# Softmax order, load order and fp16 channel matmuls in a vision-transformer tower on one core

## The chip, the core and the metric

One NeuronCore of a Trainium2 chip runs the whole program. The metric is the device time of one execution in microseconds; lower is better. The kernel before was run three times: 1566.47, 1568.02 and 1568.35 us, median 1568.02.

## The reference

Sixty-four images of 2 x 104 x 104 pixels become 170 tokens each (169 patches and a class token) of 128 channels. All of it is float32:

```
normed = (concat(x, 4 shifted copies) - mean) * rsqrt(var + EPS)      # per image
h = conv(normed * gamma + beta, W, stride 8) + b ; cls token in front
x_enc = layernorm(h)
m = relu(gcn(x_enc, W1, b1))          # graph over 128 channels, 1 -> 4 channels
g = gcn(m, W2, b2)                    # 4 -> 4 channels
h = h + concat(x_enc, g) @ Wp.T + bp
h = h + ffn(layernorm(h))             # causal attention with 2 heads, then 8 gated experts
```

The program folds the second graph convolution and the four channels of Wp into one 128 x 512 matrix (`gcn_m`), so the graph part is: one product with the adjacency, four ReLUs (one for each channel, with its own scale and bias), and a sum of one product with Wp's plain part and four products with `gcn_m`.

## The kernel before

**Tiles.** The 64 images are 16 groups (`G`) of 4 images (`NB`). A group is T = 680 token columns on 128 partitions (channels). Matmul operands are mostly split in two fp16 parts, high and low, and a product is three fp16 passes (high x high, high x low, low x high); a matmul over 680 columns is two instructions of 340 (helper `both`, L764). The products with `gcn_m` are float32 (L764 too; operand `h1`, four ReLU outputs of 680 columns).

**Stages.** A first stage (until about 162 us) loads the images, multiplies 65 times with gamma on VectorE (L1217), convolves in 65 steps on TensorE (L751) and, woven between by the step numbers in `FIRST_0`, `GRAPH_0`, `QK_0` and `FIRST_1`, does the chains of groups 0 and 1 up to their attention. Then for each group follow `attention(g)` and `ffn(g)`. The experts run in 32 slots (`SLOTS`) and three slots behind (`LAG`): slot s does `experts_in(s)` (6 matmuls, L979), and `experts_out(s - 3)` (6 matmuls, L998). ScalarE writes a GELU and, in three slots of four, its fp16 high part (L625, L630). VectorE computes the low part (L1388; in every fourth slot also the high part, L1386), and after every fourth `experts_out` it weighs the expert's output with the gate (`weigh`, L1401), whereupon GpSimd adds it to the output in DRAM by an accumulating DMA (L458). `experts_out` of the next expert waits for `weigh`'s two halves (`half_ready`, `tmp_ready`).

**Order.** Each engine runs its own program in order, written out by hand: the dictionaries at the top of the file name the slot in which a step of the next groups is done (`LN2_SLOTS`, `QK_SLOTS` for group g+1, `EARLY_SLOTS` for group g+2). In slots 28 to 31 ScalarE does the four ReLUs (L546) of group g+2. In slots 31 to 34 TensorE does the attention values of group g+1 (L876), which ScalarE copies out of PSUM (`values_evac`, L579).

**Attention before.** TensorE: values, scores 0 (images 0 and 1, L891 and L895), `plain` and channel 0, scores 1, channels 1 and 2, then transposes (`turn_probs`, L906), channel 3, `weigh` (L918, probabilities times values), `project` (L925), `mean2`, gate logits (L961). VectorE: maxima 0 and 1 (L1295, L1298), `normalise` of each image (L1303, L1310), `turned` (L1317, the copy of transposed probabilities), `h2` (L1263, the sum of the graph part into the tokens), `y_parts`, `dev2`. ScalarE: 16 exponentials (L589), four for an image. The last group's attention has no graph part of a next group beside it (`ahead` is false).

**Loads.** SP loads the first images (`all0`, `all1`) and `pack_b`, ScalarE's queue `edge` and `pack_a` (gamma and the convolution's weights). In the first group GpSimd also splits the weights of experts 4 to 7 (`split`, L422 and L424), each time ahead of the accumulating DMA.

## Time and profile before

| | us |
|---|---|
| median of 3 runs | 1568.02 |
| the profiled execution, its time | 1570.0 |
| its span, first to last instruction | 1568.2 |
| first stage, until the first scores | about 164 |
| the period of one group in the middle | 87.73 |
| the last attention and its experts | about 85 |

In that execution TensorE is busy for 1489.1 us, VectorE 1192.9, ScalarE 1102.4 and GpSimd 191.8. The mean granted clock of TensorE is 0.985 of full speed. In the timeline a row is a run of equal instructions: start, time, engine, line, operation, output and inputs, count, and in brackets the idle time before it and what ended it. A float32 matmul shows as two records. Ends of matmuls are modelled, so the distance between starts is the better measure of TensorE's pace.

### The profile page before, as it was taken

To read this page: it belongs to the slowest core of one execution; us is meant where nothing else is said; L and a number is where in the kernel's file an instruction comes from. 1 tells how busy PE (TensorE), PEld (TensorE's weight loads), DVE (VectorE), ACT (ScalarE), POOL (GpSimd) and SP (SyncE) were. 2 spreads that over 40 slices of the span, in tenths; PEclk is the share of its full clock that TensorE was granted. 3 is DMA by queue.
4 is the path that set the end of the run, shared out by engine and by line. 5 is a ranking of instruction groups with operands and counts; after the bars stand their busy time and mean duration, and the time that the engine had idled before them with its cause. 6 is when DMAs were issued, how large, how long until landed. Compare 5 with 4: busy or idle time off the path is not lost.

```text
span 1568.2 us, 31340 instructions
## 1 busy us (share of the span) xinstructions
PE 1489.1 (95%) x10879; PEld 1021.1 (65%) x10879; DVE 1192.9 (76%) x2535; ACT 1102.4 (70%) x1925; POOL 191.8 (12%) x223
## 2 busy tenths in 40 slices
PE   6898999999999999999999999999999999999998
PEld 4554666666666666666666666666666666667665
DVE  6768886868778687878788787878788787877765
ACT  5232776777777777777777777787777777777766
POOL 1134041110101010110101010110101010100101
PEclk9998999999999999999999999999999999999979
DMA  7866043433333242433333242433333242433334
GB/s 237 197 152 137 25 138 46 107 45 98 38 93 48 34 109 36 107 45 98 44 89 47 43 97 36 107 44 98 44 98 44 55 83 32 108 43 101 53 90 54
DMA packets 40196, 125.55 MB, mean 80 GB/s; under 512 B 5728, under 2 KB 5728, under 8 KB 37984
## 3 DMA queue, kind: packets, MB, share of 16 engines
q0 software_dynamic: 22464, 55.81, 25.4%
q1 hardware_dynamic: 17408, 68.52, 12.6%
q10 hardware_dynamic: 288, 0.77, 0.1%
q8 instruction: 19, 0.31, 0.1%
q14 instruction: 17, 0.14, 0.0%
HBM read 68.98 MB, written 50.48 MB: 76 GB/s over the span
## 4 chain that ended last, share of the span: by engine, by line
PE 52%; DVE 23%; issue 6%; ACT 2%; DVEq 1%; DMA 1%; POOL 0%; POOLq 0%; ACTq 0%
PE pair L998 20%; PE pair L979 17%; PE pair L764 5%; DVE area L1388 5%; DVE area L1310 3%; PE pair L891 2%; DVE root_t L1230 2%; DVE area L1317 2%; DVE area L1401 2%; PE pair L925 1%; PE pair L918 1%; DVE area L1386 1%; PE pair L876 1%; PE pair L845 1%; PE pair L792 1%
## 5 line engine op out<-in xcount | busy, mean ns | idle before, releaser
L625 ACT ACTIVATE area<-pair,pack_b_sb 128x680 f32<-128x680 f32 x512 | 422.5, 828 | 225.9 <-PE pair L979 221.5
L1388 DVE TENSOR_TENSOR area<-area 128x680 f16<-128x680 f32 x512 | 444.7, 872 | 145.1 <-ACT area L630 140.3
L998 PE MATMUL pair<-area,ws 128*128 128x340 f16 x3072 | 529.9, 307 | 16.4 <-DVE area L1401 15.5
L979 PE MATMUL pair<-area,ws 128*128 128x340 f16 x3072 | 527.9, 308 | 0.0
L998 PEld LDWEIGHTS pair<-area,ws 128*128 128x128 f16 x3072 | 284.8, 98 | 172.1 <-DVE area L1401 47.3
L979 PEld LDWEIGHTS pair<-area,ws 128*128 128x128 f16 x3072 | 297.8, 98 | 143.8
L630 ACT ACTIVATE area<-pair,pack_b_sb 128x680 f16<-128x680 f32 x384 | 316.1, 823 | 0.0
L458 POOL DMA_DIRECT2D tower_out<-area x128 | 109.3, 854 | 1182.1 <-DVE area L1401 1112.4
L1401 DVE SCALAR_TENSOR_TENSOR area<-pair,pack_b_sb,area 128x340 f32<-128x340 f32 x256 | 133.9, 565 | 31.7 <-PE pair L998 23.0
L589 ACT ACTIVATE area<-pair,nbias,root 85x85 f32<-85x85 f32 (+1 forms) x256 | 112.3, 463 | 21.5 <-DVE nbias L1298 21.5
L751 PE MATMUL pair<-area,pack_a_sb 128*128 128x392 f32 (+1 forms) x260 | 95.9, 514 | 17.5 <-DVE area L1217 14.4
L751 PEld LDWEIGHTS pair<-area,pack_a_sb 128*128 128x128 f32 x260 | 50.8, 205 | 54.6 <-DVE area L1217 26.6
L1386 DVE CAST area<-area 128x680 f16<-128x680 f32 x128 | 67.3, 526 | 20.9 <-ACT area L625 15.5
L764 PE MATMUL pair<-area,gcn_m 128*128 128x340 f32 x256 | 81.6, 451 | 0.0
L1295 DVE TENSOR_REDUCE mx<-pair 85x4 f32<-85x340 f32 x64 | 41.0, 680 | 46.0 <-PE pair L895 46.0
L546 ACT ACTIVATE area<-pair,pack_b_sb 128x680 f32<-128x680 f32 x64 | 59.1, 934 | 16.6 <-PE pair L764 16.0
L1217 DVE TENSOR_TENSOR area<-area,pack_a_sb 128x728 f32<-128x728 f32 x65 | 61.7, 995 | 0.3 <-PE pair L751 0.3
L906 PE MATMUL pair<-ident,area 85*85 85x85 f32 x384 | 45.6, 257 | 13.2 <-DVE area L1310 13.2
L1310 DVE TENSOR_SCALAR area<-area,rs 85x85 f32<-85x85 f32 (+1 forms) x256 | 55.6, 278 | 2.3
L764 PEld LDWEIGHTS pair<-area,gcn_m 128*128 128x128 f32 x256 | 46.0, 190 | 17.0
L526 ACT ACTIVATE ht<-pair 128x392 f32<-128x392 f32 (+1 forms) x26 | 19.8, 874 | 50.1 <-PE pair L751 50.1
L589 ACT ACTIVATION_READ_ACCUMULATOR area<-pair,nbias,root 85x1 f32 x256 | 54.2, 212 | 0.0
(209 smaller groups left out, 1615.3 us busy)
## 6 DMA issues: line engine op xcount, KB each, us to landing
tower_out<-area POOLq DMA_DIRECT2D x128, 340.0 KB, 4.6
area<-gate_scratch SPq DMA_DIRECT2D x16, 1360.0 KB, 10.0
area<-gate_scratch SPq DMA_DIRECT2D x16, 1020.0 KB, 7.2
area<-cells SPq DMA_DIRECT2D x16, 392.0 KB, 5.2
area<-cells POOLq DMA_DIRECT2D x14, 392.0 KB, 6.5
area<-area POOLq DMA_DIRECT2D x14, 392.0 KB, 4.8
tower_out<-ht SPq DMA_DIRECT2D x16, 340.0 KB, 2.3
area<-gate_scratch SPq DMA_DIRECT2D x16, 340.0 KB, 4.8
```

Source lines behind the costliest of these rows:

```text
L458: pool.dma_start(out[:, g * T:(g + 1) * T], tmp[e % 2], accum_op=ALU.add).then_inc(out_done, 16)
L589: nc.scalar.activation(probs[:, b * SCORE + o0:b * SCORE + o0 + w], score_ps_at(b)[:, h, c * QC:c * QC + w], ACT.Exp, bias=nbias[:, n:n + ...
L625: nc.scalar.activation(two(hid[slot % NHID]), halves(hid_ps[slot % 2]), ACT.Gelu_apprx_tanh, bias=col(COL_B1 + slot)).then_inc(hid_ready, 1)
L630: nc.scalar.activation(two(hh[slot % NPART]), halves(hid_ps[slot % 2]), ACT.Gelu_apprx_tanh, bias=col(COL_B1 + slot)).then_inc(hhi_act, 1)
L751: last = mm(cells_ps(p, j), conv_w[:, shift * D:(shift + 1) * D], xg[n % XG][:, c0 * BZ:c1 * BZ], start=(shift == 0), stop=(shift == SHIFT ...
L764: last = mm(fr_ps[:, j, 0:TH], lhs, rhs[:, j, :], start=start, stop=stop)
L979: last = mm(hid_ps[slot % 2][:, j, 0:TH], lhs[:, w], rhs[:, j * TH:(j + 1) * TH], start=(i == 0), stop=(i == 2))
L998: last = mm(eo_ps[:, j, 0:TH], lhs[:, w], rhs[:, j * TH:(j + 1) * TH], start=(m % CH == 0 and i == 0), stop=(m % CH == CH - 1 and i == 2))
L1310: last = v.tensor_scalar(p, p, rs[:, n:n + 1], None, ALU.mult)
L1386: v.tensor_copy(hh[slot % NPART], hid[slot % NHID]).then_inc(hhi_dve, 1)
L1388: v.tensor_tensor(hl[slot % NPART], hid[slot % NHID], hh[slot % NPART], ALU.subtract).then_inc(hlo_ready, 1)
L1401: v.scalar_tensor_tensor(tmp[e % 2][:, j * TH:(j + 1) * TH], eo_ps[:, j, 0:TH], b2_s[:, e:e + 1], gbc[:, e * T + j * TH:e * T + (j + 1) * ...
```

## The change

1. The four channels' products are three fp16 passes over `gcn_h`, `gcn_l` (a new split of `gcn_m`, VectorE, once) and `h1_h`, `h1_l`. ScalarE writes a ReLU to one of two buffers (`relu`), and VectorE makes the high part and the low part of it (steps `part0` to `part3`).
2. Scores 0 and 1 of the next group are computed in slots 32 and 33, VectorE's maxima too; the values come after `plain` and channel 0, into another PSUM pair (`eo_ps`), and VectorE copies them out, in two copies.
3. `pack_a` is loaded in two parts on SP's queue.
4. GpSimd issues the accumulating DMA ahead of `split`.

The diff, cut to its core:

```diff
-               "relu0": 28, "relu1": 29, "relu2": 30, "relu3": 31}
+               "relu0": 28, "relu1": 29, "relu2": 30, "relu3": 31,
+               "part0": 29, "part1": 30, "part2": 31}
 FIRST_0 = ...
-           "relu2": 19, "relu3": 19}
+           "relu2": 19, "relu3": 19, "part0": 19, "part1": 19, "part2": 20, "part3": 20}
 FIRST_1 = ...
-           "relu2": 62, "relu3": 62}
+           "relu2": 62, "relu3": 62, "part0": 62, "part1": 62, "part2": 63, "part3": 64}
-DVE_PREP = {4: 1, 6: 2, 9: 3, 17: 5, 18: 6, 20: 7, 25: 8, 28: 9}
+DVE_PREP = {4: 1, 6: 2, 9: 3, 17: 5, 18: 6, 20: 7, 21: 8, 25: 9, 28: 10}
+        h1_h, h1_l = (h1[:, 2 * n * T:2 * (n + 1) * T].bitcast(F16) for n in range(2))
+        relu = [xh, sqq]
 # SP
+            sp.dma_start(gam, pack_a[:, 0:SHIFTS * NP * NP]).then_inc(gam_in, 16)
             sp.dma_start(all0, first0).then_inc(all0_in, 16)
+            sp.dma_start(conv_w, pack_a[:, SHIFTS * NP * NP:]).then_inc(conv_w_in, 16)
             sp.dma_start(all1, first1).then_inc(all1_in, 16)
 # GpSimd, weigh
+                    pool.dma_start(out[:, g * T:(g + 1) * T], tmp[e % 2], accum_op=ALU.add).then_inc(out_done, 16)
                     if g == 0 and e + 4 < E:
                         split(e + 4)
-                    pool.dma_start(out[:, g * T:(g + 1) * T], tmp[e % 2], accum_op=ALU.add).then_inc(out_done, 16)
 # ScalarE
-            act.dma_start(packs["pack_a"][:, :], pack_a).then_inc(pack_a_in, 16)
+                    if later or c >= 2:
+                        act.wait_ge(relu_lo, 4 * g + c - 1)
-                    nc.scalar.activation(two(h1[:, c * T:(c + 1) * T]), halves(fr_ps), ACT.Relu,
+                    nc.scalar.activation(two(relu[c % 2]), halves(fr_ps), ACT.Relu,
-                for b in range(NB):
-                    values_evac(g, b, later)
+                if later:
+                    act.wait_ge(tmp_ready, g * E - 1)
 # TensorE, graph
-                    last = both(gcn_m[:, step * D:(step + 1) * D], two(h1[:, step * T:(step + 1) * T]),
-                                start=False, stop=(step == 3))
+                    pe.wait_ge(relu_lo, 4 * g + step + 1)
+                    both(gcn_h[:, w], two(h1_h[:, src]), start=False, stop=False)
+                    both(gcn_h[:, w], two(h1_l[:, src]), start=False, stop=False)
+                    last = both(gcn_l[:, w], two(h1_h[:, src]), start=False, stop=(step == 3))
 # TensorE, values
                 if b == 0 and later:
-                    pe.wait_ge(hhi_act, his(g, 0) - 1)
+                    pe.wait_ge(half_ready, g * E)
                 if b == 2 and later:
-                    pe.wait_ge(hhi_act, his(g, 0))
+                    pe.wait_ge(tmp_ready, g * E)
 # TensorE, scores
-                pe.wait_ge(vp_ready, g * NB + 2 * m + 2)
+                if later:
+                    pe.wait_ge(hhi_act, his(g, 0) - 1 + m)
+                elif m == 1:
+                    pe.wait_ge(img_step[1], 3)
 # TensorE, turn_probs
-                elif later:
-                    pe.wait_ge(tmp_ready, g * E)
+                else:
+                    pe.wait_ge(vp_ready, 2 * g + b + 1)
 # TensorE, attention
-                for b in range(LAG if later else 0, NB):
+                if not later:
+                    for m in range(NB // 2):
+                        scores(g, m, later)
+                graph_of("plain", 0)
+                for b in range(NB):
                     values(g, b, later)
-                scores(g, 0)
-                graph_of("plain", 0)
-                scores(g, 1)
-                graph_of(1, 2)
-                turn_probs(g, 0, later)
-                turn_probs(g, 1, later)
+                graph_of(1)
+                turn_probs(g, 0)
+                turn_probs(g, 1)
+                graph_of(2)
+                weigh(g, 0)
+                turn_probs(g, 2)
+                weigh(g, 1)
+                turn_probs(g, 3)
                 graph_of(3)
-                weigh(g, 0)
-                turn_probs(g, 2, later)
-                weigh(g, 1)
-                turn_probs(g, 3, later)
                 weigh(g, 2)
 # TensorE, slots 32 to 34
-                    else:
-                        values(g + 1, slot - SLOTS, True)
+                    elif slot - SLOTS < NB // 2:
+                        scores(g + 1, slot - SLOTS, True)
 # VectorE
+                if step[:4] == "part":
+                    c = int(step[4])
+                    half = slice(c * T, (c + 1) * T)
+                    dve.wait_ge(h1_ready, 4 * g + c + 1)
+                    v.tensor_copy(h1_h[:, half], relu[c % 2]).then_inc(relu_hi, 1)
+                    dve.wait_ge(relu_hi, 4 * g + c + 1)
+                    v.tensor_tensor(h1_l[:, half], relu[c % 2], h1_h[:, half], ALU.subtract).then_inc(relu_lo, 1)
+            def values_out(g, k):
+                dve.wait_ge(vp_ps, g * NB + 2 * k + 2)
+                v.tensor_copy(vp[:, k * 4 * D:(k + 1) * 4 * D], eo_ps[0:QC, k, :]).then_inc(vp_ready, 1)
             def attention(g, later, ahead):
-                maxima(g, 0)
-                maxima(g, 1)
+                if not later:
+                    for m in range(NB // 2):
+                        maxima(g, m)
                 normalise(g, 0)
                 normalise(g, 1)
+                values_out(g, 0)
+                values_out(g, 1)
+                normalise(g, 2)
                 turned(g, 0)
-                normalise(g, 2)
                 turned(g, 1)
                 normalise(g, 3)
+                if ahead and later:
+                    early(g + 1, "part3")
+                turned(g, 2)
+                turned(g, 3)
                 if ahead:
                     graph(g + 1, "h2")
-                turned(g, 2)
-                turned(g, 3)
 # VectorE, slots 32 and 33, after expert_slot
+                    if successor and 0 <= slot - SLOTS < NB // 2:
+                        maxima(g + 1, slot - SLOTS)
```

In `experts` on VectorE the wait for `hid_ready` is moved into the branch that needs it.

## Rows read from the trace of the kernel before

**Rows 1.** The page: busy time of each engine.

```profile
PE 1489.1 (95%) x10879; PEld 1021.1 (65%) x10879; DVE 1192.9 (76%) x2535; ACT 1102.4 (70%) x1925; POOL 191.8 (12%) x223
```

**Rows 2.** Windows: stretch, length, busy PE, PEld, DVE, ACT, POOL; clock, DMA, GB/s.

```profile
698.28:786.01 87.73, 85.31 (x660) 59.14 (x659) 68.19 (x148) 66.10 (x116) 8.31 (x10) 1.00 0.34 68
...
240.00:250.00 10.00, 7.63 (x42) 4.35 (x40) 5.85 (x9) 4.51 (x7) 1.70 (x2) 0.83 0.41 54
1488.00:1508.00 20.00, 18.77 (x96) 12.56 (x96) 10.99 (x36) 10.03 (x27) 0.00 (x0) 0.52 0.01 1
```

**Rows 3.** Chain that ended last, in order of time: six fp16 matmuls.

```profile
293.11 0.87 PE pair L998 x6
```

**Rows 4.** Timeline of PE, one attention in the middle.

```profile
698.99 1.30 PE L764 MATMUL pair<-area,gcn_m 128*128 128x340 f32 x4
700.23 1.12 PE L891 MATMUL pair<-area 64*85 64x85 f32 x16
...
709.97 0.66 PE L918 MATMUL pair<-area 85*64 85x170 f32 x8 [0.33 <-DVE area L1317]
...
715.08 1.89 PE L979 MATMUL pair<-area,ws 128*128 128x340 f16 x12
```

**Rows 5.** Timeline of DVE, the same attention.

```profile
690.03 0.87 DVE L1388 TENSOR_TENSOR area<-area 128x680 f16<-128x680 f32 x1 [1.91 <-ACT area L630]
690.81 1.05 DVE L1401 SCALAR_TENSOR_TENSOR area<-pair,pack_b_sb,area 128x340 f32<-128x340 f32 x2
...
698.32 1.28 DVE L1295 TENSOR_REDUCE mx<-pair 85x4 f32<-85x340 f32 x2 [1.09 <-PE pair L895]
...
703.25 0.17 DVE L1303 RECIPROCAL rs<-sm 85x4 f32<-85x4 f32 x1
...
704.24 0.17 DVE L1303 RECIPROCAL rs<-sm 85x4 f32<-85x4 f32 x1
...
709.25 1.27 DVE L1317 COPY area<-pair 85x510 f32<-85x510 f32 x2
```

**Rows 6.** Timeline of ACT, the same attention: high part, first and last exponential.

```profile
693.62 0.87 ACT L630 ACTIVATE area<-pair,pack_b_sb 128x680 f16<-128x680 f32 x1
...
699.83 0.42 ACT L589 ACTIVATE area<-pair,nbias,root 85x85 f32<-85x85 f32 x1 [1.30 <-DVE nbias L1298]
...
706.33 0.52 ACT L589 ACTIVATE area<-pair,nbias,root 85x170 f32<-85x170 f32 x1
```

**Rows 7.** Timeline of DVE, first stage.

```profile
55.84 0.51 DVE L1255 CAST area<-area 128x680 f16<-128x680 f32 x1
56.39 0.87 DVE L1258 TENSOR_TENSOR area<-area 128x680 f16<-128x680 f32 x1
...
82.55 0.93 DVE L1263 SCALAR_TENSOR_TENSOR ht<-pair,gcn_c,ht 128x680 f32<-128x680 f32 x1 [11.06 <-PE pair L764]
...
156.12 1.58 DVE L1164 TENSOR_REDUCE statz<-area 128x56 f32<-128x784 f32 x1
...
162.90 0.22 DVE L1180 COPY statz<-pair 128x56 f32<-128x56 f32 x1 [0.99 <-PE pair L760]
```

**Rows 8.** Timeline of ACT, first stage: the four ReLUs of group 1.

```profile
158.35 3.34 ACT L546 ACTIVATE area<-pair,pack_b_sb 128x680 f32<-128x680 f32 x4 [8.71 <-PE pair L764]
```

**Rows 9.** Waits of PE, first group's experts, then those of a group in the middle.

```profile
PE pair L998 <- DVE area L1401: 5.1, 4, 2.4
...
PE pair L998 <- DVE area L1401: 0.8, 2, 0.4
```

**Rows 10.** Timeline of POOL, first group: the accumulating DMA behind the last split.

```profile
236.81 0.87 POOL L458 DMA_DIRECT2D tower_out<-area  x1
```

**Rows 11.** Timeline of ACT and PE, the last attention.

```profile
1484.21 0.42 ACT L589 ACTIVATE area<-pair,nbias,root 85x85 f32<-85x85 f32 x1 [1.30 <-DVE nbias L1298]
...
1487.25 1.16 PE L906 MATMUL pair<-ident,area 85*85 85x85 f32 x6 [3.12 <-DVE area L1310]
...
1502.10 5.26 PE L979 MATMUL pair<-area,ws 128*128 128x340 f16 x18
```

More of the change, by code:

```diff
@@ L157, in vit_tower @@
         gcn_m = sb("gcn_m", [128, 4 * D])
+        gcn_h, gcn_l = (sb(n, [128, 4 * D], F16) for n in ("gcn_h", "gcn_l"))
         gcn_c = sb("gcn_c", [128, 1])
@@ L532, in var_evac, with early @@
                                      bias=eps[0:QC, at:at + 1], scale=scale).then_inc(var_out[kind], 1)
-            def early(g, step):
+            def early(g, step, later=True):
                 if step == "tok_hi":
@@ L573, in queries_keys @@
                                          ACT.Copy).then_inc(wide_ready, 1)
-            def values_evac(g, b, later):
-                act.wait_ge(vp_ps, g * NB + b + 1)
-                if b == 0 and later:
-                    act.wait_ge(tmp_ready, g * E - 1)
-                nc.scalar.activation(vp[:, b * 2 * D:(b + 1) * 2 * D], hid_ps[b // 2][0:QC, b % 2, 0:2 * D],
-                                     ACT.Copy).then_inc(vp_ready, 1)
             def exps(g, b):
@@ L645, in chain @@
                 for step in steps_in(FIRST_0, n):
-                    early(0, step)
+                    early(0, step, later=False)
                 for step in steps_in(GRAPH_0, n):
@@ L727, in conv_first @@
             def conv_first():
+                pe.wait_ge(conv_w_in, 16)
                 for shift in range(SHIFTS):
@@ L867, in values @@
                 if b == 0 and later:
-                    pe.wait_ge(hhi_act, his(g, 0) - 1)
+                    pe.wait_ge(half_ready, g * E)
                 if b == 2 and later:
-                    pe.wait_ge(hhi_act, his(g, 0))
-                if b == 3 and not later:
-                    pe.wait_ge(img_step[1], 3)
+                    pe.wait_ge(tmp_ready, g * E)
+                if b == 0 and not later:
+                    pe.wait_ge(tok_done, 2 * NP)
                 for k in range(2):
@@ L875, in values, with scores @@
                     for n, (x_part, w_part) in enumerate(((xh_h, wv_h), (xh_l, wv_h), (xh_h, wv_l))):
-                        last = mm(hid_ps[b // 2][0:QC, b % 2, k * D:(k + 1) * D],
+                        last = mm(eo_ps[0:QC, b // 2, (2 * (b % 2) + k) * D:(2 * (b % 2) + k + 1) * D],
                                   x_part[:, t * QC:(t + 1) * QC], w_part[:, :], start=(n == 0), stop=(n == 2))
                 last.then_inc(vp_ps, 1)
-            def scores(g, m):
+            def scores(g, m, later):
                 if m == 0:
                     pe.wait_ge(kn_ready, g + 1)
-                pe.wait_ge(vp_ready, g * NB + 2 * m + 2)
+                if later:
+                    pe.wait_ge(hhi_act, his(g, 0) - 1 + m)
+                elif m == 1:
+                    pe.wait_ge(img_step[1], 3)
                 for b in (2 * m, 2 * m + 1):
@@ L897, in scores, with turn_probs @@
                 last.then_inc(score_ps, 1)
-            def turn_probs(g, b, later):
+            def turn_probs(g, b):
                 pe.wait_ge(p_ready, g * NB + b + 1)
@@ L1383, in experts @@
                 else:
+                    dve.wait_ge(hid_ready, n + 1)
                     if slot >= NPART:
```

18 lines of the change are left out of this document (11 added, 7 removed).

## The prediction

> **What bounds the kernel now.** I read the page first: TensorE is busy for 95% of the span, VectorE for 76%, ScalarE for 70% [rows 1]. The windows show why that is nearly the whole story in the middle: a group takes 87.73 us, TensorE works in 85.31 of them at full clock, VectorE in 68.19 [rows 2]. So a shorter product on TensorE looks like time won. But the share is a mean over a group, and the products with `gcn_m` stand in the attention, where TensorE, VectorE and ScalarE hand each other work. There the timeline is the view to read. The probabilities' path ends in `weigh` of image 2, which TensorE starts at 709.97 after an idle 0.33, ended by VectorE's copy L1317 [rows 4, 5]. So before the change the attention's last part is paced by VectorE already; from `weigh` of image 2 the next group's first slot follows in 5.11 us (715.08) [rows 4].
>
> **Part 1, TensorE's channels.** Two float32 matmuls (four records) occupy TensorE from 698.99 to 700.23, 1.24 us [rows 4]; six fp16 matmuls take 0.87 [rows 3]. Four channels save 4 x 0.37 = 1.48 us of TensorE in a group.
>
> **Part 2, VectorE's new work in a middle group.** A cast to fp16 and the subtraction behind it: the subtraction starts 0.55 after the cast (55.84 to 56.39) [rows 7], and L1388, the same operation, lets its successor start after 0.78 (690.03 to 690.81) [rows 5]. So one `part` is 1.33 us, four are 5.32. The copies of the values: a copy of 85x510 from PSUM takes 1.27 for two, started 0.60 apart [rows 5]; two copies of 85x512 come to 1.20. ScalarE loses four smaller copies, which isn't worth anything: it isn't the late one.
>
> Now the order, from VectorE's L1388 of slot 29, which starts at 690.03 after waiting for ScalarE [rows 5] and doesn't move. From there VectorE has in the changed program, in this order: low part 29 (0.78), part0 (1.33), the gate weighing of expert 6 (1.05 less the overlap, 0.97), low part 30 (0.78), part1 (1.33), low part 31 (0.78, its input is there at 694.49 [rows 6]), part2 (1.33), two maxima (1.28 and the small L1298, 1.45 each), the weighing of expert 7 (0.97), normalise 0 (0.99, from 703.25 to 704.24 [rows 5]), normalise 1 (0.99), values (1.20), normalise 2 (0.99), turned 0 and 1 (1.20), normalise 3 (0.99), part3 (1.33). That sums to 18.86, and with 0.3 of waiting for the exponentials (below) to 19.16: 709.2. Channel 3 on TensorE waits for part3, whose last instruction ends some 0.1 after its successor can start, takes 0.87, and `weigh` of image 2 is behind it in TensorE's queue: 709.2 + 0.1 + 0.87 = 710.15, against 709.97. The copy of image 2's transposed probabilities, 0.68 from 709.2, is hidden beside channel 3.
>
> ScalarE's exponentials in that order: maxima 0 start at 697.3, the first exponential at about 698.85 instead of 699.83, and the 16 take 7.0 (699.83 to 706.33 + 0.52) [rows 6]. They are ready for normalise 1 about 0.3 late, for 2 and 3 early. TensorE: `experts_out` of slot 28 waits for the weighing of expert 6, which is now 1.33 later; this costs it about 1.0, but its last experts still end near 699.0, ahead of VectorE's weighing of expert 7 (700.2), so this wait is covered by VectorE's chain. The whole saving of 1.48 goes the same way: TensorE waits for VectorE. **Per group +0.2**, and there are 14 attentions of that form: **+2.8**. Bounds: a group might gain 0.5 (the 0.3 of waiting and some overlaps gone) or lose 0.5 (each of some ten hand-overs 0.05 dearer): -7 to +7.
>
> **Part 3, the first stage.** Group 1's parts stand in steps 62 to 64. VectorE now reaches part0 at 156.12 (where L1164 stood), but the ReLUs only begin at 158.35 and the first ends near 159.2 [rows 7, 8]: 3.1 idle, and then the 5.3 of the parts. What was at 162.90, the start of the image factors, behind which stand group 0's maxima and exponentials, comes 8.4 later. In the attention of group 0 the two copies of values stand ahead of normalise 2, with some slack: +0.8. **+9.2** (7 to 11). Group 0's parts (5.3) and the split of `gcn_m` (about 1.1, by columns between the smaller casts and a part) stand in steps 19 to 21. There VectorE waits 11.06 for the graph's products [rows 7], which covers them; but ReLU 2 and 3 wait for parts, ScalarE's copy of convolved tokens is behind them, and TensorE's next step behind that; TensorE gets 1.5 back in the channels: **+1** (0 to +3). The split load lets VectorE start its first product when the one-hot work is over: **-0.3** (0 to -0.3).
>
> **Part 4, the order on GpSimd in group 0.** TensorE waits 5.1 us for L1401 in group 0's experts, in a middle group 0.8 [rows 9]; L1401 waited for the accumulating DMA (the last one issued at 236.81 [rows 10]) behind the splits. The stall before 243.58 also brought a stretch at half clock (granted clock 0.83 from 240 to 250, so 3.4 us at 1.2 GHz, [rows 2]), which costs 1.7. Issued first, the DMAs are done when the weighing needs them, and the splits, one expert each, still end ahead of their slots: 4.3 and 1.7, less a little that stays, **-5.8** (-4 to -6).
>
> **Part 5, the last attention.** No parts are in it. Scores 0 come in slot 32, so the exponentials begin 4.1 earlier than 1484.21 [rows 11], but the weighing of expert 7 and the values' copies (2.2) stand before normalise 2, so the last normalise ends 2.5 earlier. The stretch behind it runs at half clock before (0.52 from 1488 to 1508 [rows 2]) and, with a gap of the same kind, I take it to do so again: **-2.5** (0, if the gap is longer, to -6.5, if the clock stays at 2.4 GHz).
>
> **Sum**: +2.8 + 9.2 + 1.0 - 0.3 - 5.8 - 2.5 = +4.4. Against the profiled execution (1570.0, span 1568.2) that is 1574.4; against the median 1568.02, which is 2.0 lower, 1572.4.
>
> **The rivals.**
> *TensorE sets the pace (faster).* Place: the attention of the 14 middle groups; price -1.48 each, -20.7, and with the other terms (+1.6) 1548.9. It decides where VectorE's chain from 690.03 to part3 is shorter than about 17.5 us. For it: the exponentials start 1.0 earlier, and VectorE has 19.5 us free in a group [rows 2]. Against: these are in the slots, not in this stretch. A part of it, 0.4 to 0.8 in a group, gives 1558 to 1564. Chance of the whole 0.07, of the part 0.17.
> *The terms nearly cancel (no change).* A middle group at -0.1 and a cheaper first stage: 1566 to 1571. Chance 0.26.
> *The forecast*, slower by 3 to 10: 0.38.
> *The clock falls in each attention.* TensorE now has gaps of about 1.0 at the wait for expert 6, before the first transposes and before channel 3, and its last attention shows what half clock costs: from the first exponential to the first slot 17.89 (1484.21 to 1502.10 [rows 11]), in the middle 15.25 (699.83 to 715.08 [rows 4, 6]) with channel 3 and the second mean in it, two float32 products of 1.24 each that the last doesn't have; so 2.6 to 5.1 more in a group. All 14: +36 to +71, 1608 to 1643; three of them, 1580 to 1588. Against: in the middle the clock is 1.00 throughout, and the stretches that fell had a longer gap before them (3.12, and 2.4 at 243.58 [rows 9, 11]). The Trainium skill, TensorE: Matmul & The Clock Gate, section "A second HAM failure mode: psum-queue depth-cycling", says that small idles between groups of matmuls can by themselves make the clock swing between its levels; by that rule this rival would hold, and the trace before shows no such swing at the gaps of 0.3 and 0.4 that it has [rows 4, 9]. Chance 0.05.
> *The order on GpSimd brings nothing*, since the weights' transfers or VectorE's slower work beside the splits still hold the weighing: +5.8 on the forecast, 1578.2. For it: L1401 stalls in that group four times, not once [rows 9]. Chance 0.07.
>
> **The numbers.** What a measurement of this kernel can tell from no change is 0.2%, 3.1 us. Likeliest is 1572.4. The range 1560 to 1584 takes in -7 to +7 of the middle groups with two or three of the other bounds; it leaves out the whole of the first rival, the clock and a little of the rest. Faster 0.24, same 0.26, slower 0.50 (0.38 + 0.05 + 0.07).
>
> **What would show it.** The period between two groups' first channels: 87.9. TensorE's busy time some 20 less, its idle time in the attentions more, with waits for VectorE's part3 ahead of channel 3 and for L1401 in slot 31. VectorE busy about 100 more, without a gap between slot 29 and `h2`. Image factors at about 171 instead of 162.90. No DMA wait of L1401 in group 0 and no half clock at 245. The last first slot at about 2.5 less its distance from the scores. I am wrong if the period is under 87.3 or over 88.3, or if the clock is under 1.00 in middle groups.

## The result and the profile after

Both kernels were timed side by side, the changed one in two batches. The first gave 1584.97 us (4 executions, 1580.63 to 1587.62) against 1568.18, a ratio of 1.0106 [1.0081, 1.013]; the second, the run `e9_changed_again` below, 1583.39 us (6 executions) against 1567.91, 1.0097 [1.0079, 1.0115]. **The change makes the kernel 1% slower**, some 16 us. I had forecast slower, but by 4.4 us, with an upper end of 1584: the sign was right, the size was not; the median of the first batch lies outside the range, that of the second just inside it. One execution of the kernel before took 2312.73 us at a mean granted clock of 0.608, in the batch beside e1 to e4, and is left out of every ratio.

The page of the changed kernel (busy time of each engine, the granted clock in 40 slices, the engines' shares of the chain that ended last; first line of it as in [rows 1]):

```profile
PE 1480.1 (93%) x11007; PEld 1008.7 (64%) x11007; DVE 1291.6 (81%) x2697; ACT 1089.1 (69%) x1861; POOL 195.3 (12%) x223
...
PEclk9998799999999999999999999999999999999979
...
PE 48%; DVE 34%; issue 9%; ACT 7%; DVEq 1%; DMA 1%; ACTq 0%; POOLq 0%
```

TensorE is busy 9 us less (I had said some 20), VectorE 99 us more, most of it the parts, as forecast. A group in the middle (window; columns as in [rows 2]):

```profile
726.57:814.41 87.84, 84.26 (x667) 58.13 (x667) 74.11 (x159) 65.21 (x111) 8.44 (x9) 1.00 0.34 68
```

87.84 us against 87.73, TensorE 1.05 us less of it, VectorE 5.92 us more, the clock at 1.00. So the middle, where the change was meant to work, is level. The 16 us are elsewhere. I cut both traces at the same events and compare what lies between (in brackets the kernel before's length); the second profile of the changed kernel (`e9`) shows which differences come back.

| stretch | predicted | changed - before | e9 - before |
|---|---|---|---|
| start to the product of the edges, group 1 (before 156.40) | +0.7 | +2.0 | -1.3 |
| from there to the image factors (6.50) | +8.4 | +8.5 | +8.6 |
| to the first exponential of group 0 (5.10) | 0 | +1.4 | +1.4 |
| to the first expert slot of group 0 (14.80) | +0.8 | **+8.1** | **+5.3** |
| to the next group's `plain` (76.78) | -5.8 | -2.1 | -0.1 |
| 13 groups (1140.39) | +2.8 | +1.4 | +1.3 |
| last `plain` to the last first slot (102.13) | -2.5 | -2.1 | -1.6 |
| to the end (66.1) | 0 | +0.4 | -0.3 |
| sum (span 1568.2; 1585.8; 1581.6) | +4.4 | +17.6 | +13.4 |

**The row of VectorE in the middle**, timeline of DVE, an attention of the changed kernel; it is the one that I added up step by step:

```profile
707.32 0.87 DVE L1417 TENSOR_TENSOR area<-area 128x680 f16<-128x680 f32 x1 [1.90 <-ACT area L632]
708.10 0.51 DVE L1276 CAST area<-area 128x680 f16<-128x680 f32 x1
708.64 0.87 DVE L1278 TENSOR_TENSOR area<-area 128x680 f16<-128x680 f32 x1
709.43 1.04 DVE L1430 SCALAR_TENSOR_TENSOR area<-pair,pack_b_sb,area 128x340 f32<-128x340 f32 x2
...
719.75 0.17 DVE L1323 RECIPROCAL rs<-sm 85x4 f32<-85x4 f32 x1 [0.28 <-ACT area L591]
...
725.65 0.87 DVE L1278 TENSOR_TENSOR area<-area 128x680 f16<-128x680 f32 x1
726.43 1.27 DVE L1337 COPY area<-pair 85x510 f32<-85x510 f32 x2
```

From 707.32 to 726.43 are 19.11 us; my sum was 19.16, with the one wait of 0.3 in it that stands here as 0.28. TensorE in the same attention, with its waits:

```profile
710.05 1.08 PE L1008 MATMUL pair<-area,ws 128*128 128x340 f16 x6 [0.88 <-DVE area L1430]
...
721.57 1.19 PE L914 MATMUL pair<-ident,area 85*85 85x85 f32 x12 [0.94 <-DVE area L1349]
...
726.57 0.75 PE L766 MATMUL pair<-area,gcn_h 128*128 128x340 f16 x4 [0.43 <-DVE area L1278]
727.16 0.45 PE L766 MATMUL pair<-area,gcn_l 128*128 128x340 f16 x2
727.54 0.66 PE L926 MATMUL pair<-area 85*64 85x170 f32 x8
```

Channel 3 waits for part3, and `weigh` of image 2 starts 20.22 us after VectorE's 707.32, where [rows 4, 5] have 19.94. The shorter products on TensorE are all given back in these three waits.

**The first attention**, timeline of PE and the windows over it:

```profile
179.91 0.45 PE L766 MATMUL pair<-area,gcn_l 128*128 128x340 f16 x2
185.32 1.99 PE L914 MATMUL pair<-ident,area 85*85 85x85 f32 x12 [4.96 <-DVE area L1349]
...
202.78 1.89 PE L989 MATMUL pair<-area,ws 128*128 128x340 f16 x12
```

```profile
185.00:190.00 5.00, 4.68 (x27) 3.35 (x27) 3.94 (x14) 3.46 (x12) 0.00 (x0) 0.50 0.00 0
190.00:195.00 5.00, 5.00 (x30) 3.49 (x30) 1.37 (x2) 0.54 (x1) 0.00 (x0) 0.50 0.01 2
195.00:200.00 5.00, 5.00 (x21) 3.05 (x22) 1.78 (x3) 1.00 (x2) 0.00 (x0) 0.50 0.00 0
```

TensorE stands idle for 4.96 us, and then works at 1.2 GHz nearly up to the first expert slot, without a gap, while VectorE and ScalarE wait for it. In the kernel before the clock is 1.00 from 165 to 185. The experiment e5 below says how much of the +8.1 this is: 7.0.

### The profile page after: what moved, and what is told of

It reads as the page before. It is cut to its first block, busy times and chain, and to the rows that moved or that the text cites. A ratio compares the mean times of both kernels' runs of the same rounds, so it can differ in the third digit from the quotient of the medians.

```text
span 1585.8 us, 31507 instructions
## 1 busy us (share of the span) xinstructions
PE 1480.1 (93%) x11007; PEld 1008.7 (64%) x11007; DVE 1291.6 (81%) x2697; ACT 1089.1 (69%) x1861; POOL 195.3 (12%) x223
## 4 chain that ended last, share of the span: by engine, by line
PE 48%; DVE 34%; issue 9%; ACT 7%; DVEq 1%; DMA 1%; ACTq 0%; POOLq 0%
PE pair L1008 16%; PE pair L989 15%; DVE area L1417 8%; PE pair L766 5%; ACT area L591 3%; PE pair L753 3%; DVE area L1430 3%; DVE area L1330 2%; DVE root_t L1243 2%; DVE area L1276 2%; PE pair L926 2%; ACT area L632 2%; DVE area L1415 2%; PE pair L933 2%; DVE area L1278 1%
## 5 line engine op out<-in xcount | busy, mean ns | idle before, releaser
L1417 DVE TENSOR_TENSOR area<-area 128x680 f16<-128x680 f32 x512 | 444.4, 870 | 118.0 <-ACT area L632 113.1
L1430 DVE SCALAR_TENSOR_TENSOR area<-pair,pack_b_sb,area 128x340 f32<-128x340 f32 x256 | 134.0, 565 | 15.6 <-PE pair L1008 15.3
L753 PE MATMUL pair<-area,pack_a_sb 128*128 128x392 f32 (+1 forms) x260 | 99.3, 526 | 26.4 <-DVE area L1230 22.0
L605 ACT ACTIVATE area<-pair 128x340 f32<-128x340 f32 x32 | 14.5, 454 | 71.5 <-PE pair L933 71.5
L1278 DVE TENSOR_TENSOR area<-area 128x680 f16<-128x680 f32 x64 | 55.5, 867 | 2.2
L914 PEld LDWEIGHTS pair<-ident,area 85*85 85x85 f32 x384 | 36.2, 164 | 29.3 <-DVE area L1330 25.6
L766 PE MATMUL pair<-area,gcn_h 128*128 128x340 f16 x256 | 48.9, 313 | 6.0 <-DVE area L1278 6.0
```

The source lines that it names most:

```text
L753: last = mm(cells_ps(p, j), conv_w[:, shift * D:(shift + 1) * D], xg[n % XG][:, c0 * BZ:c1 * BZ], start=(shift == 0), stop=(shift == SHIFT ...
L766: last = mm(fr_ps[:, j, 0:TH], lhs, rhs[:, j, :], start=start, stop=stop)
L1417: v.tensor_tensor(hl[slot % NPART], hid[slot % NHID], hh[slot % NPART], ALU.subtract).then_inc(hlo_ready, 1)
L1430: v.scalar_tensor_tensor(tmp[e % 2][:, j * TH:(j + 1) * TH], eo_ps[:, j, 0:TH], b2_s[:, e:e + 1], gbc[:, e * T + j * TH:e * T + (j + 1) * ...
```

## The experiments

The kernel before and the changed one, each with one part undone, left out or added; every run timed beside the kernel before. In the diffs - is the kernel that the experiment starts from.

| run | starts from | us | ratio to the kernel before | middle group |
|---|---|---|---|---|
| e1_order_f32 | changed | 1546.41 | 0.9867 [0.9842, 0.9893] | 86.03 |
| e2_load_order | before | 1565.08 | 0.9983 [0.9968, 0.9997] | 87.72 |
| e3_gpsimd_order | before | 1566.62 | 1.0 [0.9985, 1.0016] | 87.73 |
| e4_late_parts | changed | 1578.81 | 1.0076 [1.0054, 1.0097] | 87.83 |
| e5_filler | changed | 1577.65 | 1.0068 [1.0046, 1.009] | 87.83 |
| e6_primer | changed | 1579.05 | 1.0074 [1.0048, 1.01] | 87.82 |
| e7_no_low | changed | 1542.84 | 0.9845 [0.9821, 0.9869] | 85.64 |
| e8_order_prime_fill | e1 | 1537.90 | 0.9824 [0.9799, 0.9849] | 86.02 |
| e9_changed_again | changed | 1583.39 | 1.0097 [1.0079, 1.0115] | 87.83 |
| e10_gpsimd_low | changed | 1619.13 | 1.0315 [1.0292, 1.0338] | 88.3 to 91.6 |
| e11_scalar_high | changed | 1577.63 | 1.0063 [1.0047, 1.008] | 87.70 |
| e12_best_old_gpsimd | e8 | 1540.88 | 0.9822 [0.98, 0.9843] | 86.02 |

### Which engine's row sets a middle group

**e1_order_f32**: the order alone, the channels in fp32 again.

```diff
-                    both(gcn_h[:, w], two(h1_h[:, src]), start=False, stop=False)
-                    both(gcn_h[:, w], two(h1_l[:, src]), start=False, stop=False)
-                    last = both(gcn_l[:, w], two(h1_h[:, src]), start=False, stop=(step == 3))
+                    last = both(gcn_m[:, step * D:(step + 1) * D], two(h1[:, step * T:(step + 1) * T]),
+                                start=False, stop=(step == 3))
```

(and without the parts on VectorE, the split of `gcn_m` and the ReLUs' waits)

> The changed kernel with the four channels of the graph again one fp32 pass each (ReLUs written as fp32, no parts on VectorE), all else of the change kept: the new order of attention, the split load, the GpSimd order. Theory 1, VectorE's row of work from the reciprocal of the gates to the last part sets a middle group's length, and the parts delay the first stage: a middle group takes about 86.3 us instead of 87.84, the image factors come back to about 163, the first expert slot of group 0 to about 184, the whole to 1540 to 1548. Theory 2, TensorE sets the pace of the middle: its channels cost 0.37 us more each, a middle group takes 89.3 us, and the whole is 1575 or more.

A middle group took 86.03 us and the whole 1546.41: Theory 1, within 0.3 us a group. The two halves of the change in a middle group are now separate (the load and GpSimd's order, which e1 keeps, bear on the first stage and group 0 alone): the order gives 1.70 us a group (87.73 to 86.03), the fp16 channels take 1.80 back (86.03 to 87.83), 23 us over 13 groups. In all they take 37 us (1583.39 for e9 against 1546.41), since the first stage loses too.

**e7_no_low**: TensorE's work unchanged, VectorE's subtractions gone.

```diff
-                    v.tensor_copy(h1_h[:, half], relu[c % 2]).then_inc(relu_hi, 1)
-                    dve.wait_ge(relu_hi, 4 * g + c + 1)
-                    v.tensor_tensor(h1_l[:, half], relu[c % 2], h1_h[:, half], ALU.subtract).then_inc(relu_lo, 1)
+                    v.tensor_copy(h1_h[:, half], relu[c % 2]).then_inc(relu_lo, 1)
...
-                    both(gcn_h[:, w], two(h1_l[:, src]), start=False, stop=False)
+                    both(gcn_l[:, w], two(h1_h[:, src]), start=False, stop=False)
```

> The changed kernel without the low halves of the ReLU outputs: VectorE only casts each to fp16 (no subtraction, 4 x 0.87 us less of it per group), and the pass that read the low half reads the high half with the low weights once more, so TensorE's instructions keep their number and shape; the output leaves out the low half's product. Theory 1, VectorE's row of work sets a middle group's length: the group gets shorter by between 1.8 us (what taking all parts out gave) and 3.3 us, since TensorE's cheaper channels now count as well: 84.5 to 86.0 instead of 87.83, the whole 1545 to 1560. Theory 2, TensorE's own row sets it: 87.8 stays, and only the first stage gains, 3 us.

85.64: with as many instructions of the same shapes on TensorE a group is 2.19 us shorter, so it was VectorE's row that set the 87.83. The whole, 1542.84, is 2 us below the range that I gave for it. The waits of PE from 600 to 1300 us say where the bound goes. First the changed kernel, then e7 (what waited, for whom: us in total, times, longest):

```profile
PE pair L1008 <- DVE area L1430: 12.1, 24, 0.9
PE pair L914 <- DVE area L1349: 7.5, 8, 0.9
PE pair L794 <- DVE root L1247: 4.7, 8, 0.6
PE pair L766 <- DVE area L1278: 3.5, 8, 0.4
```

```profile
PE pair L1008 <- DVE area L1428: 5.0, 16, 0.4
PE pair L794 <- DVE root L1247: 4.7, 8, 0.6
PE pair L914 <- DVE area L1347: 2.4, 9, 0.3
```

In these 700 us TensorE is busy for 671.35 in the changed kernel, 687.12 in e7 and 689.63 in e1: the last two are near what I take for TensorE's own bound. Between them lies what the cheaper channels are worth there: 86.03 - 85.64 = 0.39 us a group and not 1.48; e7 still has the casts on VectorE, and TensorE waits 2.4 us for its copies, where e1 has no such wait.

**e11_scalar_high** and **e10_gpsimd_low** give a half of the parts to another engine.

```diff
+                    nc.scalar.activation(two(h1_h[:, c * T:(c + 1) * T]), halves(fr_ps), ACT.Relu,
+                                         bias=scal[:, 4 + c:5 + c], scale=scal[:, c:c + 1]).then_inc(relu_hi, 1)
...
-                    v.tensor_copy(h1_h[:, half], relu[c % 2]).then_inc(relu_hi, 1)
```

> The changed kernel with the high halves written by ScalarE, as a second ReLU with fp16 output, in place of VectorE's casts. Theory 1, VectorE's row alone sets the length: 4 x 0.52 us less of it, a middle group at 85.8, the whole at 1555. Theory 2, ScalarE becomes the bound at the end of the experts: slots 28 to 31 have 11 activations of 0.82 us in 6.9 us already and get 4 more, 3.3 us: a middle group at 88 to 90, the whole at 1588 or more.

87.70, neither: VectorE has 2 us less to do and the group is 0.13 us shorter. TensorE's waits in the same 700 us show where it went: those for the weighing fall from 12.1 to 7.7, but scores wait 4.2 us for ScalarE, of which the changed kernel has none, and the first transposes 8.9 instead of 7.5. As I read it, ScalarE is now as late as VectorE was. The whole is 5.8 below e9; the profiles show 2.8, of which 1.7 lie in the 13 groups.

```diff
+                    if e == 6 and ahead:
+                        for c in range(4):
+                            half = slice(c * T, (c + 1) * T)
+                            pool.wait_ge(relu_hi, 4 * (g + 2) + c + 1)
+                            pool.tensor_tensor(h1_l[:, half], relu[c % 2], h1_h[:, half], ALU.subtract).then_inc(relu_lo, 1)
```

> The changed kernel with the low halves of the ReLU outputs subtracted by GpSimd instead of VectorE from group 2 on (behind the accumulating DMA of expert 6), groups 0 and 1 as they were. Theory 1, only VectorE's own row of work counts: a middle group falls from 87.83 us to the 85.64 that leaving the subtractions out gave, the whole to 1555. Theory 2, VectorE's small and large operations slow down while GpSimd computes on the same memory, as its roots did in group 0 (0.17 to 0.19 us each alone, up to 1.40 us beside the splits): a middle group takes 87 us or more, and the whole 1574 or more.

Theory 2, and worse than it said: 1619.13. The timelines of POOL and of DVE at one place in the middle:

```profile
724.13 1.78 POOL L473 TENSOR_TENSOR area<-area 128x680 f16<-128x680 f32 x1
726.38 1.47 POOL L473 TENSOR_TENSOR area<-area 128x680 f16<-128x680 f32 x1 [0.46 <-DVE area L1281]
729.71 1.47 POOL L473 TENSOR_TENSOR area<-area 128x680 f16<-128x680 f32 x1 [1.86 <-DVE area L1281]
```

```profile
724.05 2.25 DVE L1281 CAST area<-area 128x680 f16<-128x680 f32 x1
728.33 0.87 DVE L1423 TENSOR_TENSOR area<-area 128x680 f16<-128x680 f32 x1 [2.04 <-ACT area L637]
729.12 0.51 DVE L1281 CAST area<-area 128x680 f16<-128x680 f32 x1
```

GpSimd's subtraction takes 1.47 us instead of 0.87, VectorE's cast beside it 2.25 instead of 0.51, and with two ReLU buffers ScalarE waits for GpSimd and VectorE for ScalarE (2.04): a ring of three engines in place of two. TensorE waits 16.7 us for ScalarE in the same 700, up to 2.1 at a time, where the changed kernel has no such wait. But the slower operations alone are not the 36 us. Two groups of e10, columns as in [rows 2]:

```profile
914.47:1002.81 88.34, 83.96 (x669) 58.15 (x667) 71.63 (x152) 63.46 (x105) 14.20 (x13) 1.00 0.34 67
1002.81:1094.38 91.57, 85.94 (x668) 58.72 (x666) 74.15 (x158) 66.68 (x120) 14.20 (x13) 0.98 0.32 65
```

Only two of the 13 groups keep the clock at 1.00, and they take 88.34 and 88.42, some 0.5 more than in the changed kernel; the others, at 0.96 to 0.98, take 89.80 to 91.57. So GpSimd's subtractions cost some 7 us over the 13 groups, and some 28 more come with the granted clock, which the changed kernel has at 1.00 there. What the rival "the clock falls in each attention" was about is seen here, beside waits of 2.1 us instead of 0.9.

### The first attention and the first stage

**e5_filler**: the idle time filled, and nothing else.

```diff
                 graph_of(1)
+                if not later:
+                    for n in range(60):
+                        mm(fr_ps[:, n % 2, TH:TH + 170], wqk_h[:, 0:D], wqk_h[:, 0:170], start=False, stop=False)
                 turn_probs(g, 0)
```

> The changed kernel with 60 extra fp16 matmuls of 170 columns on TensorE in attention 0, between channel 1 of group 1 and the first transposes, where TensorE stood idle for 4.96 us at 185.32; their results go into unused columns and are never read. Theory 1, the granted clock of 0.50 from 185 to 201 follows that idle time, and costs some 7 us: with the gap filled the clock stays at 1.00 there, the first expert slot comes at about 195.5 instead of 202.78, the whole takes 1577 to 1579. Theory 2, attention 0 is long for another reason (VectorE's order, the values copies): the slot stays at 202 to 204 and the whole at 1585.

```profile
178.42 4.56 PE L955 MATMUL pair<-wqk_h 128*128 128x170 f16 x60
183.06 1.25 PE L914 MATMUL pair<-ident,area 85*85 85x85 f32 x12
...
193.53 1.75 PE L992 MATMUL pair<-area,ws 128*128 128x340 f16 x11
```

The idle time is gone, the clock is 1.00 in every 5 us from 175 to 195, and from the first transposes to the first expert slot it takes 10.47 us (183.06 to 193.53) instead of 17.46 (185.32 to 202.78): 7.0 us for 60 matmuls whose results nobody reads. Against e9 it is 4.2, as its clock was back at 2.4 GHz after some 10 us and the other profile's after some 17. The whole is 1577.65, 5.7 below e9. Theory 1.

How much the half clock costs varies, though. From the first exponential to the first expert slot it takes 14.80 us in the kernel before, 22.93 and 20.14 in the two profiles of the changed one, and 15.94 in e5, near my 15.6. The same instructions stand in this attention in e7, e10 and e11, with idle times of 5.07, 4.18 and 5.08, and there it takes only 17.35, 17.35 and 17.68, since the clock is back within a few microseconds. In e7, timeline of PE and windows:

```profile
176.10 1.73 PE L914 MATMUL pair<-ident,area 85*85 85x85 f32 x12 [5.07 <-DVE area L1347]
```

```profile
175.00:180.00 5.00, 3.90 (x24) 2.81 (x26) 4.65 (x16) 4.23 (x15) 0.00 (x0) 0.66 0.00 0
180.00:185.00 5.00, 5.00 (x51) 3.56 (x48) 2.46 (x4) 1.05 (x3) 0.00 (x0) 1.00 0.00 0
```

So the filling is worth 1.4 to 7.0 us by the profile that it is compared with, and why the clock comes back sooner in some was not found. The whole's 5.7 alone would not show it: e6, which doesn't fill, is 4.3 below e9. The gap comes with the new order and not with the fp16 passes: e1 has one of 4.49, and 18.03 us.

**e6_primer**: the table load ahead of the waits.

```diff
             def attention(g, later, ahead):
+                if not (later and ahead):
+                    nc.scalar.activation(primer_e[:, int(later):int(later) + 1], eps[0:1, 0:1], ACT.Exp)
                 if later:
```

> The changed kernel with a one-element exponential on ScalarE ahead of its waits in the first and in the last attention, so that the load of the exponential's table is issued before ScalarE waits for the maxima. Theory 1, the load (1.28 us at 178.56, behind nbias) is on the path in both places since ScalarE no longer copies the values: the first exponential starts 1.3 us sooner in each, the whole takes 1582.4. Theory 2, the load was overlapped anyway: no change that can be told.

Timeline of ACT at the first attention, the changed kernel and e6:

```profile
178.56 1.28 ACT L591 ACT_TABLE_LOAD   x1 [4.78 <-DVE nbias L1318]
179.85 0.42 ACT L591 ACTIVATE area<-pair,nbias,root 85x85 f32<-85x85 f32 x1
```

```profile
174.87 1.28 ACT L610 ACT_TABLE_LOAD   x1
176.17 0.20 ACT L610 ACTIVATE primer_e<-eps 1x1 f32<-1x1 f32 x1
179.56 0.42 ACT L592 ACTIVATE area<-pair,nbias,root 85x85 f32<-85x85 f32 x1 [3.19 <-DVE nbias L1321]
```

From the image factors to the first exponential 5.10 us instead of 6.46, from the last `plain` to the last attention's first exponential 79.63 instead of 80.90: 1.36 and 1.27, as expected. Not all of it arrives: from the last `plain` to the last first slot e6 takes 99.67, the changed kernel 100.08 and 100.52. The whole is 4.3 below e9, more than the two loads can give; e6's own executions run from 1575.79 to 1584.30.

**e4_late_parts**: parts 2 and 3 of group 1 into the attention.

```diff
-           "relu2": 62, "relu3": 62, "part0": 62, "part1": 62, "part2": 63, "part3": 64}
+           "relu2": 62, "relu3": 62, "part0": 62, "part1": 62}
...
                         maxima(g, m)
+                    early(g + 1, "part2")
...
-                if ahead and later:
+                if ahead:
                     early(g + 1, "part3")
```

> The changed kernel with parts 2 and 3 of group 1 taken out of the steps 63 and 64 and put into attention 0, part 2 behind the maxima and part 3 where later groups have it. Theory 1, VectorE is the last in steps 62 to 64 and idle in attention 0: image factors 2.65 us sooner (170.7), the whole 2.6 us less, 1582.4, plus or minus what a clock window shifts. Theory 2, the parts are as costly in attention 0, and nothing changes.

Edges to image factors 12.90 us instead of 15.02 and 15.13, so 2.1 to 2.2 less, and the whole 4.6 below e9. But e6 and e10, with the parts where they were, have 14.25 and 14.26: against them it is 1.35. And from the first exponential to the first slot e4, with its two parts there, takes 18.04, more than the 17.35 to 17.68 of e7, e10 and e11. Nearer to Theory 1, with the size open: between 0.7 and 2.2 us.

**e2_load_order** and **e3_gpsimd_order**: one part of the change each, on the kernel before.

```diff
+            sp.dma_start(gam, pack_a[:, 0:SHIFTS * NP * NP]).then_inc(gam_in, 16)
             sp.dma_start(all0, first0).then_inc(all0_in, 16)
+            sp.dma_start(conv_w, pack_a[:, SHIFTS * NP * NP:]).then_inc(conv_w_in, 16)
...
-            act.dma_start(packs["pack_a"][:, :], pack_a).then_inc(pack_a_in, 16)
```

> The kernel before with the split load of the first pack alone. Theory 1, the load stood at the front of the first stage and all 1.8 us by which the changed kernel's step 18 is earlier come through: 1566.2 to 1566.8. Theory 2 (the prediction's), only the 0.3 us between the two waits counts: 1567.9, no change that can be told.

A ratio of 0.9983, that is 2.7 us (0.5 to 5.0 by its interval); in its trace the products of the edges come 1.04 and 1.14 us sooner (groups 0 and 1), in the other kernels with this load group 0's 0.7 to 2.2, but for e6 and e10 where it comes 1.0 to 1.3 later. Nearer to Theory 1: the load is on the path. The timeline of DVE at the very start shows how, first the kernel before, then e2:

```profile
5.21 0.17 DVE L1068 CAST edge_f<-edge_i 128x16 f32<-128x16 int32 x1 [5.21 <-DMA edge_i<-edge]
5.41 3.22 DVE L1071 TENSOR_SCALAR stage_sb<-stage_sb,edge_f 128x128 f16<-128x128 f32 x16
8.93 3.04 DVE L1125 TENSOR_TENSOR ws<-ws,pack_a_sb 128x1352 f32<-128x1352 f32 x2 [0.29 <-DMA pack_a_sb<-pack_a]
```

```profile
4.41 0.17 DVE L1070 CAST edge_f<-edge_i 128x16 f32<-128x16 int32 x1 [4.41 <-DMA edge_i<-edge]
...
7.76 3.04 DVE L1127 TENSOR_TENSOR ws<-ws,pack_a_sb 128x1352 f32<-128x1352 f32 x2
```

The wait of 0.29 for the pack is gone, as forecast; but the edge list, ahead of it, also lands 0.80 sooner, now that ScalarE's queue has no large load behind it, and VectorE's one-hot work starts with it. 0.29 + 0.80 is about what group 0's edges come sooner. In all 12 profiles with this load the edge list is there by 4.38 to 4.68, in the two with the old one at 5.21 and 5.46. The 1.1 us are seen in the trace; the rest of the 2.7 is not explained by it.

```diff
+                    pool.dma_start(out[:, g * T:(g + 1) * T], tmp[e % 2], accum_op=ALU.add).then_inc(out_done, 16)
                     if g == 0 and e + 4 < E:
                         split(e + 4)
-                    pool.dma_start(out[:, g * T:(g + 1) * T], tmp[e % 2], accum_op=ALU.add).then_inc(out_done, 16)
```

> The kernel before with GpSimd's accumulating DMA ahead of its weight split in group 0, and nothing else. The prediction: 5.8 us less, 1562.2, and no wait of TensorE on VectorE's weighing over 2 us. What the changed kernel's profile suggests: the excess of group 0's experts over a middle group falls by 3 us only, since VectorE's small operations slow down beside the splits, 1565.

1.0 [0.9985, 1.0016]: no difference that can be told. The waits of PE in group 0's experts in e3, where the kernel before has 5.1, 4, 2.4 [rows 9]:

```profile
PE pair L998 <- DVE area L1401: 5.3, 3, 4.4
```

The four waits of a DMA's length are gone, and one of 4.4 has come. The timeline of DVE ahead of it, the roots of queries and keys, in e3 and (old order) in e2:

```profile
204.86 1.14 DVE L1227 TENSOR_SCALAR root<-root_in 85x32 int32<-85x32 int32 x1
...
207.49 1.19 DVE L1234 SCALAR_TENSOR_TENSOR root<-root_t,root 85x32 f32<-85x32 f32 x1
```

```profile
207.55 0.17 DVE L1229 TENSOR_SCALAR root<-root_in 85x32 int32<-85x32 int32 x1
...
208.20 0.19 DVE L1236 SCALAR_TENSOR_TENSOR root<-root_t,root 85x32 f32<-85x32 f32 x1
```

The splits now run at the same time as the roots (POOL from 200.96 to 210.5 in e3), and these small operations take up to 1.19 us instead of 0.19: seven of them 5.6 us instead of 1.4. In e2, with the old order, GpSimd is done with its split at 205.7, ahead of them. From group 0's first slot to the next `plain` e3 takes 77.61 us, with a half clock at 210 to 220 behind the wait of 4.4, and the kernel before 76.78, with one at 240 to 250; e2, with none, takes 73.62.

### The best version

**e8_order_prime_fill** puts together what gained: e1's order with fp32 channels, e6's early table load, e5's filling, and 94 such matmuls in the last attention. **e12_best_old_gpsimd** is e8 with GpSimd's old order.

```diff
                 graph_of(1)
+                if not later:
+                    filler(60, False)
+                if not ahead:
+                    filler(40)
...
                 graph_of(2)
+                if not ahead:
+                    filler(18)
```

(and 18 more in the place of channel 3, 18 in that of `mean2`)

> The kernel of the first experiment (the new order, channels in one fp32 pass) with the table load ahead of the waits as in the sixth and the filled gap of the fifth, and with filling matmuls in the last attention too, where no following group's graph keeps TensorE busy (94 of them, in the places of the channels). If the half clock of both attentions goes: 1546.4 less 2.6 for the two loads, less some 2 in attention 0 (it had two windows only at 170 to 180) and less 4 to 8 in the last (clock 0.50 from 1467 to 1485): 1534 to 1538. If filling does not hold the clock: 1543 to 1546.

> The kernel of the eighth experiment with GpSimd's order in group 0 as before the change (split ahead of the accumulating DMA). If the new GpSimd order brings nothing or loses a microsecond or two beside VectorE's roots, as the third experiment suggests: 1536 to 1538, the first expert slot of group 0 to the next group's plain in 74 us instead of 75.31. If it was worth something and only the clock hid it: 1540 to 1543.

1537.90 and 1540.88, ratios of 0.9824 and 0.9822: 1.8% (27 to 30 us) faster than the kernel before, and 43 to 45 us faster than e9. GpSimd's order makes no difference here either. The clock is 1.00 in the whole last attention (e8, 1452 to 1472 us; e1, 1462 to 1482, below it):

```profile
1452.00:1472.00 20.00, 19.59 (x222) 16.34 (x220) 13.40 (x43) 11.27 (x37) 0.86 (x1) 1.00 0.13 19
```

```profile
1462.00:1482.00 20.00, 16.07 (x107) 11.85 (x108) 11.24 (x36) 9.37 (x34) 0.94 (x1) 0.64 0.13 18
```

but this is worth little: from the first exponential to the last first slot 18.36 us against 19.59 in e1, and 1.2 behind it. As I read it, VectorE and ScalarE set the pace there, and a slower TensorE mostly fills its idle time. I had expected 4 to 8. In the first attention 60 matmuls are too many here: the transposes behind them begin 6.6 us after the first exponential, where e1's begin 5.5 after it, and the first slot comes 17.5 after it instead of 18.0.

## Why the prediction was right and wrong

**Part 1 and 2, the middle: right.** The step that VectorE's chain from slot 29 to part3 sets the time, and TensorE's 1.48 us are lost in waits, held to 0.05 us in its length and 0.1 in a group (+0.1 where I said +0.2; e7 shows that VectorE's row sets it, e1 what the two halves are worth). "TensorE sets the pace" falls with e7, whose group shortens by 2.19 us without any change on TensorE. What I did not see: the sum of two nearly equal terms. The order gains 1.70, the parts cost 1.80; I added VectorE's whole new row without asking what it would be with one of the two halves, and the answer, 22 us, was the more useful one.

**Part 3, the first attention: a step that failed.** The arithmetic of the parts was right: "comes 8.4 later" was measured as 8.5 and 8.6. Wrong was the sentence behind it, "In the attention of group 0 the two copies of values stand ahead of normalise 2, with some slack: +0.8". The two profiles have +8.1 and +5.3, of which the filling takes away 7.0 and 4.2 and leaves 1.1: the new order moves scores, the graph's first two channels and the values ahead of the exponentials, so that TensorE has nothing left while ScalarE computes them, 4.96 us, and comes back at 1.2 GHz. I had this gap in my own terms, as "a gap of the same kind" in Part 5, and priced it only there. I looked at the rival of the clock in the middle groups, whose gaps are 0.4 to 0.9 us and whose clock stayed at 1.00, and not at the one attention ahead of them. The rule that I named with that rival (the Trainium skill, TensorE: Matmul & The Clock Gate, section "A second HAM failure mode: psum-queue depth-cycling") did not hold here for the middle of the changed kernel: three gaps under 1 us in each attention, and no swing. In e10, with gaps of 2.1 and 1.0 us, 11 of 13 groups have stretches at half clock.

Also in Part 3: the table load, 1.4 us here and 1.3 in the last attention. Before, ScalarE's copies of the values stood ahead of the exponentials, and the load was issued while VectorE computed the maxima; I counted these copies as "not worth anything". And the load order, "-0.3 (0 to -0.3)", came to 1.0 less in e2's trace and 2.7 by its times: I saw the wait for the pack, and not that the one-hot work ahead of it waits for another load, on the queue that the change empties.

**Part 4, GpSimd's order: the other step that failed, -5.8 forecast, nothing measured in e3, -2.1 and -0.1 in the changed kernel.** I took the 4.3 us of TensorE's waits as gone once the DMAs came first. In their place came one wait of 4.4, behind VectorE's roots, slowed from 1.4 to 5.6 us beside the splits. This is the rival that I gave 0.07, "VectorE's slower work beside the splits". The half clock at 240 to 250 that I counted at 1.7 us isn't tied to the old order: e2, with that order, hasn't got it, and e3, with the new, has one at 210 to 220, e9 one at 230 to 240.

**Part 5: -2.5 forecast**, -2.1 and -1.6 measured, with the table load (+1.3) in it; the clock was at 0.50 from 1510 to 1525, as taken.

So the error of 13.2 us against the profiled execution (17.6 for 4.4) is: +7.3 in the first attention, +3.7 in GpSimd's order, +1.4 for the table load, +1.3 ahead of the edges, +0.1 for the parts, +0.8 in the last two stretches, -1.4 in the middle. In e9 it is 9.0, and the order of the two is turned: +5.7 in GpSimd's order, +4.5 in the first attention, +1.4 for the table load, -2.0 ahead of the edges. The two steps together carry the miss. With either of them right the median would have been inside the range; no bound of it had the clock in the first attention. That the second batch's 1583.39 lies inside is the width of the range and not a better account.

One thing stays open: the first 160 us. The same kernel has the product of group 1's edges at 158.37 in one profile and 155.14 in the other, and e4, e5, e6 and e10, which differ from it only later, from 156.01 to 160.21, and the half-clock stretches of the convolutions (65 to 80, 105, 130, 150 to 160) lie differently in each. Executions of the kernel before spread from 1561.23 us at a mean clock of 0.989 to 1572.14 at 0.984. What decides this was not tried.

## What to carry to other kernels

When a product on one engine is made cheaper by work on a second, add up the second engine's row between two fixed events, as VectorE's 19.1 us here, before anything else; and when two changes come together, do it for each alone. Then look at every copy of the pattern outside the loop: the first attention had the same instructions as the middle ones but nothing around them to fill TensorE's wait, and it cost more than all 13 middle groups. The granted clock belongs into such a comparison: the same instructions behind the same gap took from 17.4 to 22.9 us, so one profile doesn't price it. An instruction that seems free may be where a table load hides, and an engine that seems idle (GpSimd) may cost another one more than it takes over.

## What the hardware showed

- After 4.96 us of idle time TensorE worked at 1.2 GHz for some 17 us, after 4.59 us in e9 for some 10, though it had no gap in them; after 5.07 us in e7 the clock was 0.66 for one window of 5 us and then 1.00. 60 fp16 matmuls of 170 columns (4.56 us) in the idle time kept 2.4 GHz.
- In the middle, waits of 0.4 to 0.9 us left the clock at 1.00. Waits of 2.1 to 2.4 us went either way: in e10 one of 2.09 at 909.78 stands beside a clock of 0.68 (910 to 915), one of 2.09 at 999.70 beside 1.00, and in the changed kernel one of 2.34 at 236.61 beside 1.00.
- A half clock costs what TensorE is needed for: 7.0 us of 17.5 in the first attention, where its products stood one behind the other, and 2.4 of some 17 in the last (e1 against e8).
- VectorE's operations on 85x32 elements take 0.17 to 0.19 us, and up to 1.19 us beside GpSimd's splits in e3 (1.40 in the changed kernel at 231.59, beside a GpSimd subtraction); a cast of 128x680, 0.51 us, took 2.25 beside GpSimd's subtraction.
- The exponential's table load, 1.28 us, came behind the first exponential's wait in the changed kernel's first and last attention (178.56 and 1498.85), and ahead of that wait in its middle ones (713.54, with the exponential at 716.10) and in the kernel before (164.70, with the exponential at 168.00). Why was not found; a one-element exponential ahead of the waits took it off the path in e6.
